# Source one-hots of a window's loop turn, moved from GpSimd to VectorE and ScalarE

## What is computed

```python
def sage(h, src, dst, deg_inv, W_self, W_neigh, b):
    agg = segment_sum(h[src], dst, num_segments=1250)
    return h @ W_self + (agg * deg_inv[:, None]) @ W_neigh + b
...
deg_inv = 1 / maximum(segment_sum(ones, dst), 1)
h = relu(sage(layernorm(x), ..., W_self0, W_neigh0, b0))
x = x + sage(h, ..., W_self1, W_neigh1, b1)
hid = square(relu(layernorm(x) @ W_fc.T))
x = x + spikes(hid @ W_proj.T)          # 5 steps, mean of the spikes
```

## Time and profile before

| | us |
|---|---|
| timed runs: median of three (lowest, highest) | 1813.36 (1810.3, 1817.68) |
| profiled execution: time of the run | 1819.27 |
| profiled execution: span of the instructions | 1817.1 |

### The profile page before, as it was taken

One profiled execution on the slowest core, in us unless ns is written; L12 is line 12 of the kernel. 1 busy time (PEld: TensorE's weight loads), 2 busy tenths in 40 slices (PEclk: granted clock), 3 DMA queues, 4 the chain that ended last, 5 costly groups with the idle time before them and its releaser, 6 DMA issues.

```text
span 1817.1 us, 21946 instructions
## 1 busy us (share of the span) xinstructions
PE 1669.6 (92%) x7761; PEld 1373.8 (76%) x7764; DVE 896.1 (49%) x1522; ACT 383.4 (21%) x594; POOL 342.4 (19%) x664
## 2 busy tenths in 40 slices
PE   3687897777989999999999999999999999999997
PEld 1455674454777888887888998899899888888884
DVE  5644444444344113224553443343344378888868
ACT  2011120000011112001131231231132123232348
POOL 7755558999000000000010000000000000000000
PEclk9978899999999999999999999999999999999998
DMA  3312122222464424535571120121121223333331
GB/s 138 128 70 84 47 70 98 99 91 91 163 235 181 179 100 179 200 133 179 190 262 66 70 92 27 66 92 46 46 92 52 109 98 117 120 114 117 113 119 44
DMA packets 55913, 205.33 MB, mean 113 GB/s; under 512 B 5330, under 2 KB 13852, under 8 KB 50340
## 3 DMA queue, kind: packets, MB, share of 16 engines
q1 hardware_dynamic: 53524, 191.76, 29.4%
q0 software_dynamic: 2320, 12.58, 1.7%
HBM read 153.85 MB, written 50.47 MB: 112 GB/s over the span
## 4 chain that ended last, share of the span: by engine, by line
PE 77%; POOL 9%; issue 6%; DVE 4%; ACT 2%; DMA 2%; POOLq 1%; SPq 0%; ACTq 0%; DVEq 0%
PE bank L1414 23%; PE bank L1433 22%; PE bank L1321 21%; PE bank L1364 8%; POOL src_hot L610 8%; PE bank L1294 1%; PE bank L1268 1%; DVE at_sum L1037 1%; ACT spikes L821 1%; POOL current L606 1%; DMA fc_raw<-w_fc 1%; DVE xt L956 1%; ACT sign L834 0%; DMA at<-at_dram 0%; ACT xt L680 0%
## 5 line engine op out<-in xcount | busy, mean ns | idle before, releaser
L1321 PE MATMUL bank<-w,xt 128*128 128x512 f32 x1920 | 475.5, 408 | 2.5 <-DVE w L971 2.5
L1414 PE MATMUL bank<-x2t,fc_w 128*128 128x384 f32 (+1 forms) x2304 | 441.4, 352 | 3.5 <-ACT relu L786 3.5
L1321 PEld LDWEIGHTS bank<-w,xt 128*128 128x128 f32 x1920 | 376.3, 198 | 84.5 <-issue 2.8
L1414 PEld LDWEIGHTS bank<-x2t,fc_w 128*128 128x128 f32 x2304 | 414.4, 189 | 28.9 <-DVE fc_w L1109 3.5
L1433 PE MATMUL bank<-pr_w,hid 128*128 128x512 f32 (+1 forms) x1824 | 418.8, 390 | 0.0
L1433 PEld LDWEIGHTS bank<-pr_w,hid 128*128 128x128 f32 (+1 forms) x1824 | 338.2, 185 | 75.5
L610 POOL TENSOR_SCALAR src_hot<-iota,current 125x128 bf16<-125x128 f16 x474 | 291.4, 628 | 32.2 <-POOL current L606 32.2
L1183 DVE TENSOR_TENSOR y<-y,bank 128x512 f32<-128x512 f32 (+1 forms) x152 | 104.2, 687 | 215.2 <-PE bank L1433 215.2
L905 DVE TENSOR_SCALAR key_hot<-iota,current 125x320 bf16<-125x320 f16 x474 | 130.8, 334 | 160.3 <-POOL current L606 159.5
L1268 PE MATMUL bank<-key_hot,src_hot 125*128 125x320 bf16 x474 | 100.7, 337 | 103.8 <-POOL src_hot L610 100.6
L1364 PE MATMUL bank<-z,at 128*128 128x512 f32 x800 | 191.5, 396 | 0.0
(11 more groups left out here) (123 smaller groups left out, 900.6 us busy)
## 6 DMA issues: line engine op xcount, KB each, us to landing
fc_raw<-w_fc SPq DMA_DIRECT2D x64, 512.0 KB, 4.5
pr_raw<-w_proj SPq DMA_DIRECT2D x64, 512.0 KB, 3.5
xt<-xt_dram SPq DMA_DIRECT2D x24, 1024.0 KB, 5.0
xt_dram<-xt SPq DMA_DIRECT2D x18, 1024.0 KB, 4.3
at<-at_dram SPq DMA_DIRECT2D x20, 640.0 KB, 5.0
part_dram<-rows SPq DMA_DIRECT2D x20, 512.0 KB, 3.8
rows<-part_dram SPq DMA_DIRECT2D x20, 512.0 KB, 4.3
rows<-x SPq DMA_DIRECT2D x18, 512.0 KB, 4.9
```

The costliest lines, as they stand in the source:

```text
L1321: ins = nc.tensor.matmul(bank[:, 2 * (u % 2) + q, :], xt[j][:, a, k, :], w[:, k, b, q * HALF:(q + 1) * HALF], start=(k == 0 and m == 0), s ...
L1414: ins = nc.tensor.matmul(bank[:, 4 + (c if g == 0 else j % 2), 0:n], fc_w[:, j % 2, k, a, :], x2t[g][:, k, v, c0:c0 + n], start=(k == 0 an ...
```

## The change

- GpSimd makes only the head set of a window (`head_of_window`): one copy, three source one-hots. `current` has one buffer.
- In each loop turn VectorE makes the source one-hots of set 1 itself, beside the key one-hots of sets 1 and 2. Its column operands come straight from `edge_col` at an address from the loop register. It now waits for `hot_used` itself.
- In each loop turn ScalarE makes the source one-hots of set 2: three squares of `column - iota` into `dist`, then one Relu of `1 - dist` over all three. It waits for its last Relu ahead of the squares, and for `dist_ready` and `hot_used` ahead of the Relu. On ScalarE the windows' one-hots stand behind `high_of_row` and ahead of the next standard deviation in A0, ahead of `copy_counts` in S0, and for window 0 between the second and the third weight cast.
- TensorE waits for `src_hot_ready` at the head set, for `act_hot_ready` at set 2, and at set 1 for the key one-hots alone, which VectorE makes last.
- In G0 `sum_at(n)` is made behind `take_aggregate(n - 1)`, `degree(n)` stands behind the first 28 products of unit n, and `inverse_degree(n)` behind the row's low part.

```diff
 HEAD_SET, LOOP_SETS = 0, (1, 2)
+ACT_SET = 2
...
+            ("current", [P, 2, SET], F32), ("src_hot", [P, 3, SET, 128], BF16),
+            ("key_hot", [P, 3, SET, WINDOW_COLS], BF16), ("dist", [P, SET, 128], BF16))
...
-        current_ready = [sem(f"current_ready{s}") for s in range(3)]
-        current_seen = [sem(f"current_seen{s}") for s in range(3)]
-        src_hot_ready = [sem(f"src_hot_ready{s}") for s in range(3)]
+        current_ready = sem("current_ready")
+        current_seen = sem("current_seen")
+        src_hot_ready = sem("src_hot_ready")
+        dist_ready = sem("dist_ready")
+        act_hot_ready = sem("act_hot_ready")
...
-            def src_one_hots(s, chunk, use):
-                nc.gpsimd.tensor_copy(current[:, s, :, :], edge_col[:, :, ds(chunk, SET)]).then_inc(current_ready[s], 1)
-                pool.wait_ge(current_ready[s], use)
-                pool.sem_inc(current_seen[s], 1)
+            def head_of_window(w, first, end):
+                pool.wait_ge(hot_used[HEAD_SET], w + 1)
+                nc.gpsimd.tensor_copy(current[:, :, :], edge_col[:, :, ds(first - SET, SET)]).then_inc(current_ready, 1)
+                pool.wait_ge(current_ready, w + 1)
+                pool.sem_inc(current_seen, 1)
                 for c in range(SET):
-                    ins = nc.gpsimd.tensor_scalar(src_hot[:, s, c, :], iota[0:P, 0:128], current[:, s, 0, c:c + 1], None,
-                                                  ALU.is_equal)
-                ins.then_inc(src_hot_ready[s], 1)
-
-            def window_of_edges(w, first, end):
-                pool.wait_ge(hot_used[HEAD_SET], w + 1)
-                src_one_hots(HEAD_SET, first - SET, w + 1)
-                with pool.Fori(first, end, LOOP_CHUNKS) as g:
-                    for i, s in enumerate(LOOP_SETS):
-                        pool.wait_ge(hot_used[s], visit)
-                        src_one_hots(s, g + SET * i, visit)
-                    pool.reg_add(visit, visit, 1)
+                    ins = nc.gpsimd.tensor_scalar(src_hot[:, HEAD_SET, c, :], iota[0:P, 0:128], current[:, 0, c:c + 1],
+                                                  None, ALU.is_equal)
+                ins.then_inc(src_hot_ready, 1)
...
+            visit = act.alloc_register("act_visit")
+            act.reg_mov(visit, 1)
+            act.sem_inc(act_hot_ready, 1)
+            registers = range_registers(act, "act")
+            ranges = [None]
+
+            def src_one_hots(v):
+
+                if v % 2 == 0:
+                    ranges[0] = load_ranges(act, registers, v)
+                first, end = ranges[0][v % 2]
+                with act.Fori(first, end, LOOP_CHUNKS) as g:
+                    act.wait_ge(act_hot_ready, visit)
+                    for c in range(SET):
+                        chunk = g + (SET * LOOP_SETS.index(ACT_SET) + c)
+                        ins = nc.scalar.activation(dist[:, c, :], iota[0:P, 0:128], ACT.Square,
+                                                   bias=edge_col[:, 0, ds(chunk, 1)], scale=-1.0)
+                    ins.then_inc(dist_ready, 1)
+                    act.wait_ge(dist_ready, visit)
+                    act.wait_ge(hot_used[ACT_SET], visit)
+                    nc.scalar.activation(src_hot[:, ACT_SET, :, :], dist[:, :, :], ACT.Relu, bias=1.0,
+                                         scale=-1.0).then_inc(act_hot_ready, 1)
+                    act.reg_add(visit, visit, 1)
+
...
-            for k in range(KD):
+            for k in range(2):
+                high_of_w(0, k)
+            act.wait_ge(edge_cols_ready, 2)
+            act.wait_ge(constants, 14)
+            act.wait_ge(range_ready, 1)
+            src_one_hots(0)
+            for k in range(2, KD):
                 high_of_w(0, k)
...
+                for k, v in WINDOW_SLOTS.get(A0 + n, []):
+                    src_one_hots(v)
                 if n + 2 < TILES:
                     standard_deviation(0, n + 2)
                 for k, v in WINDOW_SLOTS.get(A0 + n, []):
...
             for p in range(TILES):
                 for k, v in WINDOW_SLOTS.get(S0 + p, []):
+                    src_one_hots(v)
                     copy_counts(v)
...
-            def key_one_hots(v, s, use):
-                dve.wait_ge(current_ready[s], use)
+            def window_of_edges(v, first, end):
+                dve.wait_ge(current_ready, v + 1)
                 for c in range(SET):
-                    ins = nc.vector.tensor_scalar(key_hot[:, s, c, :], iota[0:P, :], float(v * WINDOW_COLS),
-                                                  current[:, s, 1, c:c + 1], ALU.add, ALU.is_equal)
-                ins.then_inc(key_hot_ready[s], 1)
-
-            def window_of_edges(v, first, end):
-                key_one_hots(v, HEAD_SET, v + 1)
+                    ins = nc.vector.tensor_scalar(key_hot[:, HEAD_SET, c, :], iota[0:P, :], float(v * WINDOW_COLS),
+                                                  current[:, 1, c:c + 1], ALU.add, ALU.is_equal)
+                ins.then_inc(key_hot_ready[HEAD_SET], 1)
                 with dve.Fori(first, end, LOOP_CHUNKS) as g:
-                    for s in LOOP_SETS:
-                        key_one_hots(v, s, visit)
+                    for i, s in enumerate(LOOP_SETS):
+                        dve.wait_ge(hot_used[s], visit)
+                        for c in range(SET):
+                            chunk = g + (SET * i + c)
+                            if s != ACT_SET:
+                                nc.vector.tensor_scalar(src_hot[:, s, c, :], iota[0:P, 0:128],
+                                                        edge_col[:, 0, ds(chunk, 1)], None, ALU.is_equal)
+                            ins = nc.vector.tensor_scalar(key_hot[:, s, c, :], iota[0:P, :], float(v * WINDOW_COLS),
+                                                          edge_col[:, 1, ds(chunk, 1)], ALU.add, ALU.is_equal)
+                        ins.then_inc(key_hot_ready[s], 1)
                     dve.reg_add(visit, visit, 1)
...
             for n in range(TILES):
                 if n >= 1:
                     take_aggregate(0, n - 1)
-                inverse_degree(n)
+                    sum_at(n)
                 if n < 2:
                     low_of_w(2, n)
                 if n >= 1:
                     low_of_row(1, n - 1)
-                if n + 1 < TILES:
-                    sum_at(n + 1)
+                inverse_degree(n)
                 if 2 <= n < KD:
                     low_of_w(2, n)
...
             def products_of_set(v, s, use, start=False):
-                pe.wait_ge(src_hot_ready[s], use)
+                if s == HEAD_SET:
+                    pe.wait_ge(src_hot_ready, use)
+                if s == ACT_SET:
+                    pe.wait_ge(act_hot_ready, next_visit)
                 pe.wait_ge(key_hot_ready[s], use)
...
                 with pe.If(few_edges):
                     for s in range(TURN_AT):
                         products(at, s, exact=False)
+                if l == 0:
+                    degree(n)
                 if n >= 1:
...
             for n in range(TILES):
-                degree(n)
                 aggregate(0, n)
```

More of the change, by code:

```diff
@@ L145, in gnn_ffn @@
         at_raw = [tile[:, :, :].bitcast(F32) for tile in at]
-        counts_tile, edge_col, iota, zero_w, current, src_hot, key_hot = put_from(
+        counts_tile, edge_col, iota, zero_w, current, src_hot, key_hot, dist = put_from(
             at_at, ("counts_tile", [128, TILES, T], F32),
             ("edge_col", [P, 2, CHUNKS + PAD_CHUNKS], F32), ("iota", [128, WINDOW_COLS], F16), ("zero_w", [P, T], F16),
-            ("current", [P, 3, 2, SET], F32), ("src_hot", [P, 3, SET, 128], BF16),
-            ("key_hot", [P, 3, SET, WINDOW_COLS], BF16))
+            ("current", [P, 2, SET], F32), ("src_hot", [P, 3, SET, 128], BF16),
+            ("key_hot", [P, 3, SET, WINDOW_COLS], BF16), ("dist", [P, SET, 128], BF16))
         (edge_int, tmp_int, key_part, dst_int, dst_rows_f, chunk_min, chunk_max, group_min, group_max, window_first,
@@ L626, in _ @@
             ranges = load_ranges(pool, first_registers, 0)
-            window_of_edges(0, *ranges[0])
+            head_of_window(0, *ranges[0])
             for k in POOL_LOW:
@@ L631, in _ @@
                                         ALU.subtract).then_inc(w_low_pool, 1)
-            window_of_edges(1, *ranges[1])
+            head_of_window(1, *ranges[1])
             with pool.Fori(1, WINDOWS // 2) as pair:
@@ L635, in _ @@
                 for i in range(2):
-                    window_of_edges(2 * pair + i, *ranges[i])
+                    head_of_window(2 * pair + i, *ranges[i])
             pool.wait_ge(pair_done, 2 * (G1 + TILES))
@@ L895, in _ @@
             dve.wait_ge(range_ready, 1)
+            dve.wait_ge(edge_cols_ready, 2)
             dve.wait_ge(constants, 14)
@@ L1260, in _ @@
             pe.reg_mov(visit, 1)
+            next_visit = pe.alloc_register("pe_next_visit")
```

(2 more changed lines are left out.)

2 lines of the change are left out of this document (removed).

## The result

The kernel after takes 1677.88 us (median of 4 runs, 1677.02 to 1680.26), the kernel before, timed beside it, 1815.52 us (4 runs, 1810.3 to 1819.06). The ratio is 0.925, 95% interval 0.922 to 0.927, so it is faster by 7.5%. The prediction was 1680 us, with a range of 1662 to 1722. The profiled execution took 1678.42 us, span 1676.4, against a span of 1817.1 before: 140.7 us less.

The account below looks back on a forecast made before the run. TensorE, busy 92%, was held mainly by waits for GpSimd's source one-hots and slow products behind them. Gains 16 + 44 + 61 + 12 = 133 us from 1819.3 give 1686, as a median 1680 us; range 1662 to 1722.

Parts of the forecast that it names:

- What bounds it: Whole kernel: TensorE, busy 92%, waits 100.6 us for GpSimd's source one-hots and 10.5 us for VectorE's `at_sum`.
- The turn: One loop turn of a window after the change: 2.0 us against 4.2, bounds 1.76 and 2.6.
- (a): Window 0, nine turns at 2.0 us ending at 38.1, then 19.9 us carried over to the transposes: gain 16 us.
- two weight lows take 6.65 us beside GpSimd's two: Behind window 0 on VectorE: this 6.65 us collision was carried over unchanged, within the 19.9 us up to the transposes.
- (b): Windows 1 to 8: 29 us from shorter windows and 15 from slow products taken back, gain 44 us.
- The rival of the clock that stays down: Multi-turn windows: TensorE still idles, the 15 us of clock gain are not won, some 5 more lost; 1700 us, chance 0.10.
- (c): Windows 11 to 39, 29 slots: 4.1 us each instead of 6.3, 3 us left for waits, gain 61 us.
- just covered: One-turn slots: the store lands 2.9 us after issue, needed 4.1 us later; 1.5 us late costs about 0.2 us.
- the rivals of a new bound: Slots: VectorE's 12 instructions or ScalarE's chain make them 4.9 us, turns in windows 0 to 8 2.6; 1714 us, chance 0.20.
- (d): First aggregate: reordered `degree` and `sum_at` remove 1.34 us of idle time and refill per unit, gain 12 us.
- 5.9 us from the profile to the median: Whole kernel: the median of timed runs, 1813.4 us, lies 5.9 under the profiled execution, so 1686 becomes 1680.
- The slower rival: Slots: ScalarE's queue as a ring, loss above a 5.9 us chain, all gains gone at 8.3; 8.8 gives 1828 us; chance 0.03.

Follow-up runs that it names:

- the run by chunk: Kernel after, with VectorE signalling buffer 1 behind each chunk and TensorE waiting for each chunk: 1676.12 us, ratio 0.924 to the kernel before.
- the second profile: The kernel after, run and profiled once more without edits: 1679.66 us, ratio 0.926 to the kernel before.
- the run with 21 more squares: Kernel after, with 21 more two-column squares in each ScalarE set, into an unread tile: 1834.92 us, ratio 1.011 to the kernel before.
- the run with more squares: Kernel after, with three more 128-column squares in each ScalarE set, into an unread tile: 1681.69 us, ratio 0.926 to the kernel before.
- the kernel with zero products: Kernel before, with six products of zeros behind each loop set of windows 0 to 8: 1803.6 us, ratio 0.993.

## Why the prediction was right, step by step

**What bounds it.** Right: of the 140.7 us, some 125 come from the waits for GpSimd and the slow products behind them, and 12.3 from the wait for `at_sum`.

**The turn.** Taken as 2.0 us, bounds 1.76 to 2.6. At full clock it is 2.0 (70.18 to 72.19). But the way there was wrong: I summed each engine's work and took the longest, 1.9 us on ScalarE. It is neither engine but the ring through buffer 1, as the run by chunk shows: 2.0 to 2.1 us instead of 2.42 at the 1.2 GHz level, 1.81 instead of 2.01 at the 2.4 level. In window 0, where three products take 0.98 us instead of 0.58, the turn is 2.42 us. Prices of single instructions were close: on VectorE the next instruction starts 0.17 us behind a source one-hot (0.16 estimated) and 0.21 behind a key one, ScalarE's squares 0.98 for three (1.0), the Relu 0.52 (0.5). The register address showed no price of its own. The Trainium skill's table ("VectorE: DVE Perf Modes", "The TRN2 errata") gave 0.29 us by estimate for 128 elements on ScalarE; the square lasts 0.39, and 0.29 is its distance to the next.

**(a) Window 0: 16 predicted, 16.2 measured (14.9 by the second profile), with the wrong path behind the window.** The window itself takes 21.93 us instead of 36.45, 14.5 of the 16.2. It closes at 43.1 us, not by 40. VectorE left it at 41.99, the sum had 38.1: 0.9 us of that is the later start, which is a row of its own in the table, the rest the turns of 2.42 us. For what follows, the sum carried over the 19.9 us that VectorE took up to the transposes; it took 17.3. But the transposes did not wait for VectorE. TensorE from the window's close on, before and then after:

```profile
59.37 2.90 PE L1321 MATMUL bank<-w,xt 128*128 128x512 f32 x6 [2.50 <-DVE w L971]
```

```profile
44.55 2.90 PE L1358 MATMUL bank<-w,xt 128*128 128x512 f32 x6 [1.27 <-DVE w L1003]
...
48.35 11.14 PE L1358 MATMUL bank<-w,xt 128*128 128x512 f32 x48
59.33 1.03 PE L1331 MATMUL bank<-ident,rows 128*128 128x128 f32 x8
```

In both kernels TensorE waits for the first weight low and then works without a pause up to the transposes; VectorE's row is ready at 57.43, 1.9 us ahead of them. The stretch from the close takes 16.3 us, 17.9 before: 1.2 less of wait, the rest in TensorE's own products (17.5 in the second profile). Two misses, turns too short and a path that TensorE did not follow, cancelled; that is luck. The collision on that path failed too, "two weight lows take 6.65 us beside GpSimd's two". The rows after, VectorE and GpSimd, against the earlier trace rows:

```profile
43.19 2.35 DVE L1003 TENSOR_TENSOR w<-w_raw,w 128x1024 fp32r<-128x1024 f32 x2
45.46 4.63 DVE L1003 TENSOR_TENSOR w<-w_landing,w 128x1024 fp32r<-128x1024 f32 x4
...
46.31 8.39 POOL L623 TENSOR_TENSOR w<-w_landing,w 128x1024 fp32r<-128x1024 f32 x2 [32.31 <-ACT w L688]
```

The two lows that took 6.65 us take 2.35. GpSimd gets its high parts only at 46.31, since those casts now stand behind ScalarE's window, and comes while VectorE is already working through its six; it is held until 50 us and pays 8.39 us for its two, which nobody waits for. I had moved the casts and kept the collision that depended on them. Only the first low of the six is worth anything to TensorE: the 1.2 us above.

**(b) Windows 1 to 8: 44 predicted, 44.7 measured.** 26.4 us from shorter windows (29 predicted: two-turn windows take 3.80 us, 2.4 less, not 2.8) and 18.3 from the clock (15 taken): here too one miss covers the other. The rival of the clock that stays down did not come, though TensorE still idles 1.1 us behind the first nine products of such a window (68.17): the clock is 1.00.

**(c) Slots: 61 predicted, 64.5 measured.** The slot of 4.1 us was worked out to 0.01 us. The 3 us held back for waits never came: the store that was "just covered" caused none. The 29 slots give 62.3 us (6.24 less 4.09 each); the other 2.2 are window 39 itself, which the sum did not count. ScalarE's cover was as said, over 1 us (some 1.5 by the ring of the run with 21 more squares); the rivals of a new bound fell by the run with more squares.

**(d) G0: 12 predicted, 12.3 measured**, alone as well as in the change.

**Not in the sum:** 2.4 us in the feed-forward part. Over the twelve profiled executions it takes 899.2 to 901.9 us, and the kernel with zero products, where it is untouched, has 899.4; so it is not the change's. The term "5.9 us from the profile to the median" was luck as well: the kernel after's profiled execution lies 0.5 us above its median. Runs of the kernel before spread over 1810 to 1822 us, those of the kernel after over 3 us. The sum for the span was 7.7 us short (133 against 140.7), and this hid it.

**The slower rival** named the right place, and its price for the slots was near: a chain of 5.8 us gives by its rule slots of 4.1 + 2.1 = 6.2. Measured are 6.5 to 6.9 in the first slots, at a granted clock of 1.00, and behind them 8.2 and 5.5 in turn, at 0.88 on the mean (347 to 487 us). Its point of return was wrong, since it counted no turn of windows 0 to 8.

## What to carry to other kernels

When work goes from one engine to two, do not take the longest of the engines' sums as the new period: write down the ring through each buffer (fill, release, use, release) and take the longest of all. If all engines idle in a turn, it is the ring, and releasing by smaller pieces shortens it, until one engine has no idle time left. Before a stretch of the old trace is carried over, look up who waits for its end: here TensorE did not. And when an instruction is moved, look up which collisions in the old trace depended on when it ran; they do not carry over as they are.

## What was not expected of the hardware

- TensorE's idle time in short waits cost half as much again later: 35.0 us in 22 waits of at most 2.0 us in windows 1 to 8 (kernel before), and 18.3 us of slow products, at a granted clock of 0.82. Six products of zeros per wait brought it back to 1.00.
- In window 0 of the change the products of 320 columns start 0.267 us apart (six in 1.78 us), which is the 1.2 GHz level; in a slot they start 0.136 us apart (nine in 1.40). The granted clock reads 1.00 in both stretches. In window 0 the durations tell, not the clock column. With the release by chunk 39 of window 0's 57 products last 0.30 us, with products of zeros most of them do, in the change none.
- VectorE and GpSimd hold each other up for whole instructions when one of them has a `tensor_tensor` with both inputs in SBUF: beside GpSimd's a VectorE one-hot of 0.3 us takes 2.45, and beside VectorE's weight lows a GpSimd one-hot of 0.6 takes 2.4 (kernel before, two from 62.8 us on). Beside GpSimd's one-hots it is a slowing only: VectorE's of 0.25 us take 0.37 and start 0.29 us apart instead of 0.17 to 0.21 (kernel after, a slot; GpSimd's three take 1.76 us). A lock held for a whole instruction would have cost VectorE 0.59 us each, so for this pair the rows don't bear out the rule that was cited above:

```profile
291.62 1.76 POOL L612 TENSOR_SCALAR src_hot<-iota,current 125x128 bf16<-125x128 f16 x3 [0.20 <-POOL current L608]
...
292.24 0.37 DVE L941 TENSOR_SCALAR src_hot<-iota,edge_col 125x128 bf16<-125x128 f16 x1
292.53 0.36 DVE L943 TENSOR_SCALAR key_hot<-iota,edge_col 125x320 bf16<-125x320 f16 x1
```

- Before, the two engines' weight lows took turns (3.34 and 3.39 us on VectorE); after, GpSimd's first was held through four of VectorE's. Why the one gives way in one case and not in the other was not tried and stays open.
